# Graph transformer layer on one core: x @ loop weights + bias made ahead for all blocks, normalising moved to ScalarE

## What is computed

```python
k, q, v = (decomp(x, node_type, comp, basis) for ...)   # 4 basis matrices, mixed by node type
kt = einsum(k, relation_att)[edge_type, src];  vt = einsum(v, relation_msg)[edge_type, src]
e = (q[dst] * kt).sum(-1) * relation_pri[edge_type] * scale
a = softmax of e over the edges of each dst
agg = segment_sum(a * vt, dst)
out = relu(decomp(agg, node_type, comp_a, basis_a) + x @ loop_weight + bias)
return layernorm(x + out)
```

## Time and profile before

| what | value |
|---|---|
| median of 3 runs | 1438.44 us (1436.06 to 1438.98) |
| profiled execution, its own time | 1433.42 us |
| its span, first to last instruction | 1431.3 us |
| mean granted TensorE clock | 0.839 of full |
| TensorE busy | 1086.9 us (76%) |
| VectorE busy | 1007.8 us (70%) |
| GpSimd busy | 950.1 us (66%) |
| ScalarE busy | 746.5 us (52%) |
| table phase, queries | to about 197 us, to about 267 us |
| groups, first and last gather | 204.4 us, 1288.7 us |
| last addition to `agg`, end of the span | 1330 us, 1431.3 us |

### The profile page before, as it was taken

One profiled execution on the slowest core, in us unless ns is written; L12 is line 12 of the kernel. 1 busy time (PEld: TensorE's weight loads), 2 busy tenths in 40 slices (PEclk: granted clock), 3 DMA queues, 4 the chain that ended last, 5 costly groups with the idle time before them and its releaser, 6 DMA issues.

```text
span 1431.3 us, 29611 instructions
## 1 busy us (share of the span) xinstructions
PE 1086.9 (76%) x6749; PEld 892.8 (62%) x6750; DVE 1007.8 (70%) x2872; ACT 746.5 (52%) x1969; POOL 950.1 (66%) x941
## 2 busy tenths in 40 slices
PE   5999978777777676767777676777666777776797
PEld 2545544566767666666676666676656666665797
DVE  4797737677777676767777676767767676776686
ACT  2767746566555455556545455555445555540342
POOL 2567527747777777777777777777777777770441
PEclk9999989888888878878778788877878787876799
DMA  5989775323333333333333333333333333331022
GB/s 137 356 335 356 306 273 164 110 59 107 107 110 105 110 105 108 101 108 105 107 109 107 108 105 105 106 107 104 106 107 104 102 106 108 107 103 34 14 79 64
DMA packets 93799, 184.47 MB, mean 129 GB/s; under 512 B 26359, under 2 KB 59624, under 8 KB 87408
## 3 DMA queue, kind: packets, MB, share of 16 engines
q0 software_dynamic: 41680, 113.71, 27.7%
q1 hardware_dynamic: 49600, 69.49, 13.6%
q10 hardware_dynamic: 2400, 0.07, 0.1%
HBM read 127.71 MB, written 56.26 MB: 129 GB/s over the span
## 4 chain that ended last, share of the span: by engine, by line
POOL 31%; PE 26%; issue 19%; DVE 11%; DMA 5%; DVEq 4%; ACT 1%; ACTq 1%; SPq 1%; POOLq 0%
POOL kv L1161 31%; PE pb L1481 5%; DVE agg L720 3%; PE pb L1643 3%; PE pb L1592 3%; PE pb L1738 3%; PE pb L1502 3%; DVEq L691 3%; DMA kv<-table,idx_now 2%; PE pb L1552 2%; PE pb L1721 2%; DMA onehot<-in_x_dram 2%; PE pb L1618 1%; DVE work L685 1%; DVE kv L439 1%
## 5 line engine op out<-in xcount | busy, mean ns | idle before, releaser
L1161 POOL DMA_INDIRECT kv<-table,idx_now x832 | 814.6, 979 | 312.8 <-issue 246.9
L1643 PE MATMUL pb<-work,onehot 128*128 128x136 f32 x1664 | 340.4, 338 | 96.7 <-DVE agg L720 64.7
L720 DVE TENSOR_TENSOR agg<-agg,pb 128x136 f32 x832 | 241.8, 291 | 201.9 <-issue 72.0
L1643 PEld LDWEIGHTS pb<-work,onehot 128*128 128x128 f32 x1664 | 282.6, 236 | 120.0 <-issue 84.5
L1321 ACT ACTIVATE work<-pb 128x512 f32<-128x512 f32 x208 | 124.0, 596 | 331.4 <-PE pb L1581 331.4
L1592 PE MATMUL pb<-q_all,work 128*128 x1664 | 272.6, 317 | 0.7 <-ACT work L1321 0.6
L1592 PEld LDWEIGHTS pb<-q_all,work 128*128 128x128 f32 x1664 | 249.7, 229 | 7.9 <-issue 6.7
L1309 ACT ACTIVATE work<-lane,neg_lane 128x128 f32<-128x128 f32 x800 | 253.0, 390 | 0.0
L577 DVE TENSOR_TENSOR work<-kv,pb 128x512 f32<-128x512 f32 x208 | 142.3, 684 | 95.4 <-DMA kv<-table,idx_now 69.1
L1581 PE MATMUL pb<-ident,onehot 128*128 128x128 f32 x832 | 158.2, 322 | 67.0 <-ACT onehot L1315 63.7
L1581 PEld LDWEIGHTS pb<-ident,onehot 128*128 128x128 f32 x832 | 114.1, 165 | 88.0 <-ACT onehot L1315 62.9
(11 more groups left out here) (197 smaller groups left out, 1188.7 us busy)
## 6 DMA issues: line engine op xcount, KB each, us to landing
table<-kv SPq DMA_DIRECT2D x49, 1024.0 KB, 5.2
kv<-table,idx_now POOLq DMA_INDIRECT x832
seg<-item_bias SPq DMA_DIRECT2D x208, 16.0 KB
kv<-in_x_dram SPq DMA_DIRECT2D x8, 384.0 KB, 5.7
onehot<-in_x_dram SPq DMA_DIRECT2D x7, 384.0 KB
kv<-in_x_dram SPq DMA_DIRECT2D x6, 448.0 KB, 3.7
out_dram<-kv SPq DMA_DIRECT2D x6, 448.0 KB
onehot<-tile_blocks POOLq DMA_DIRECT2D x1, 784.0 KB, 8.8
```

Source lines behind the costliest of these rows:

```text
L720: v.tensor_tensor(a, a, PB[banks[i // 2 % len(banks)]][:, (i % 2) * 256:(i % 2) * 256 + W], ALU.add).then_inc(s_added, 1)
L1161: pool.indirect_dma_start(out=kv[:, o:o + 2 * D], out_offset=None, in_=table, in_offset=bass.IndirectOffsetOnAxis(ap=idx_now[par][:, i:i + ...
L1643: mm = t_.matmul(PB[banks[k % len(banks)]][:, u * 256:u * 256 + W], onehot[:, o:o + P], wv[:, b % WR, h * 2 + u, :], start=True, stop=True)
```

## The change

- `item_bias8`: at block 36 of the table phase SyncE copies `item_bias` eightfold from DRAM to DRAM, so that `segments` is one transfer instead of eight.
- `hold` waits for a semaphore that is long there instead of raising one; where a raise is kept it is `hold_apart`. The four squares raise `s_squares` once.
- x is loaded for all chunks in the last group, to one half of `kv` (places of the group before the last), each chunk when its places are weighed.
- `base` = x @ loop weights + bias, for all 49 blocks in 13 groups of 4, is kept in the queries' place `q_all`. TensorE turns 4 blocks of x into bank 0, ScalarE copies them to `spread`, TensorE multiplies into bank 2, ScalarE copies to `base`. Two turns stand in the last group's last batch, 3 groups before `turn_scores`, 4 single groups between the steps of the chain, 6 among the last sums, which use 3 banks.
- In the last stage TensorE only has the turned products and the four bases. VectorE adds `base` (first instruction) and then takes the relu and adds x (second). It makes the reciprocal and a `shift` = -mean x reciprocal; ScalarE normalises (scale and bias for each node) chunk n-1 between its copies 4, 5 and 6 and after copy 0 of the next; the last chunk is shared by both engines. `yo` has two buffers.

```diff
+    item_bias8 = nc.dram_tensor("item_bias8", [ITEMS // IL, H, IL * P], f32, kind="Internal").ap()
...
+        BASES_AT = [3, 1, 1, 1, 1]
+        BASES_FIRST = sum(BASES_AT)
-        LAST_SBANKS = [4, 5, 0, 1]
+        LAST_SBANKS = [4, 5, 3]
...
         def hold(engine):
+            engine.wait_ge(s_const, 8)
+        def hold_apart(engine):
             engine.sem_inc(s_hold, 1)
...
             def residual(ch, par):
                 for h, (c0, c1) in enumerate(((0, 4), (4, CB))):
-                    dve.wait_ge(s_layer_out, ch * 2 + h + 1)
-                    v.scalar_tensor_tensor(y[par][:, c0 * D:c1 * D], PB[4 + 2 * par + h][:, 0:(c1 - c0) * D],
-                                           0.0, x3[par][:, c0 * D:c1 * D], ALU.max, ALU.add)\
-                        .then_inc(s_residual, 1)
+                    dve.wait_ge(s_block_multiplied, ch * CB + c1)
+                    yc = y[par][:, c0 * D:c1 * D]
+                    v.tensor_tensor(yc, PB[4 + 2 * par + h][:, 0:(c1 - c0) * D],
+                                    base[:, bass.ds(ch * CN + c0 * D, (c1 - c0) * D)], ALU.add).then_inc(s_summed, 1)
+                    dve.wait_ge(s_summed, ch * 2 + h + 1)
+                    v.scalar_tensor_tensor(yc, yc, 0.0, x3[:, bass.ds(ch * CN + c0 * D, (c1 - c0) * D)],
+                                           ALU.max, ALU.add).then_inc(s_residual, 1)
...
-            def normalise(ch, par):
+            def inverse(ch, par):
                 dve.wait_ge(s_deviation, ch + 1)
-                v.reciprocal(rstd, rstd).then_inc(s_inverse_deviation, 1)
+                v.reciprocal(rstd[par], rstd[par]).then_inc(s_inverse_deviation, 1)
                 dve.wait_ge(s_inverse_deviation, ch + 1)
-                after(dve, s_stored, ch, 16, 0)
-                for c in range(CB):
-                    v.tensor_scalar(yo[:, c * D:(c + 1) * D], y[par][:, c * D:(c + 1) * D],
-                                    mv[:, c, 0:1], rstd[:, c:c + 1], ALU.subtract, ALU.mult)\
+                v.scalar_tensor_tensor(shift[par], mv[:, :, 0], -1.0, rstd[par], ALU.mult, ALU.mult)\
+                    .then_inc(s_shift, 1)
...
             def stage3(ch, par, first=False, final=False):
                 if not final:
                     products3(ch + 1, 1 - par)
                 if not first:
-                    normalise(ch - 1, 1 - par)
+                    inverse(ch - 1, 1 - par)
                 residual(ch, par)
...
         # sync
-                for h in range(H):
-                    sp.dma_start(seg3[h * IL:(h + 1) * IL, :, :], rows).then_inc(s_segments[par], 16)
+                sp.dma_start(seg3, item_bias8[bass.ds(g * IH, IH), :, :]
+                             .rearrange("i h (l e) -> (h l) i e", l=IL)).then_inc(s_segments[par], 16)
...
+                if n == STARTS_OUT_AT:
+                    sp.wait_ge(s_item_starts, 16)
+                    sp.dma_start(item_bias8, item_bias.rearrange("(j a l) e -> j a (l e)", a=1, l=IL)
+                                 .broadcast_to([ITEMS // IL, H, IL * P])).then_inc(s_starts_copied, 16)
...
-            sp.wait_ge(s_weighted, (GROUPS - 1) * NBATCH)
...
+            for ch in range(CHUNKS):
+                slots = -(-(ch + 1) * CN // (2 * D))
+                sp.wait_ge(s_weighted, (GROUPS - 2) * NBATCH + -(-slots // 4))
...
         # scalar
+            def copy_base(j):
+                many = min(4, BLOCKS - 4 * j) * D
+                act.wait_ge(s_base_made, j + 1)
+                a_.activation(base[:, j * 4 * D:j * 4 * D + many], PB[2][:, 0:many], ACT.Copy).then_inc(s_base_copied, 1)
+            copy_x3(0)
+            copy_x3(1)
+            for j in range(BASES_FIRST):
+                copy_base(j)
+                copy_x3(j + 2)
             exponentials(GROUPS - 1, 0)
...
+            def normalise(ch, par, use, cs):
+                act.wait_ge(s_shift, ch + 1)
+                after(act, s_stored[par], use, 16, 0)
+                for c in cs:
+                    a_.activation(yo[par][:, c * D:(c + 1) * D], y[par][:, c * D:(c + 1) * D], ACT.Identity,
+                                  bias=shift[par][:, c:c + 1], scale=rstd[par][:, c:c + 1]).then_inc(s_normalised, 1)
...
                 for c in range(1, CB):
                     copy_products(ch, par, c)
-                    if c == 3 and not first:
-                        deviation(ch - 1)
-                    if c == XAT + 1 and not final:
-                        copy_x3(ch + 1, 1 - par)
+                    if c == 3 and use_prev is not None:
+                        deviation(ch - 1, 1 - par)
+                    if c >= 4 and use_prev is not None:
+                        k = 2 * (c - 4)
+                        normalise(ch - 1, 1 - par, use_prev, range(k, k + 2))
                 if not final:
                     copy_products(ch + 1, 1 - par, 0)
+                if use_prev is not None:
+                    normalise(ch - 1, 1 - par, use_prev, range(CB - 1, CB))
...
         # tensor
+            def make_base(j):
...
+                    pe.wait_ge(s_base_copied, j)
+                pe.wait_ge(s_xT3_copied, j + 1)
+                for u in range(min(4, BLOCKS - 4 * j)):
+                    o = PB[2][:, u * D:(u + 1) * D]
+                    t_.matmul(o, xT3[:, j % 2, u, :], Wl[:, :], start=True, stop=False)
+                    mm = t_.matmul(o, ones3, bias3, start=False, stop=True)
+                mm.then_inc(s_base_made, 1)
...
+            bases(BASES_AT[0])
             turn_scores(g, 1)
             sums(g - 1, 0, 12)
+            bases(BASES_AT[1])
             turn_ends(g)
...
             for k in range(2 * NBATCH):
                 sums(g, 1, k, LAST_SBANKS)
+                if k % 2 and made[0] < X3:
+                    bases(1)
...
-                    t_.matmul(o, xT3[par][:, c * P:(c + 1) * P], Wl[:, :], start=False, stop=False)
-                    mm = t_.matmul(o, ones3, bias3, start=False, stop=True)
```

More of the change, by code:

```diff
@@ L211, in graph_transformer_layer @@
         s3 = Space(kv, 2 * G * 2 * D)
-        x3 = [s3.take(CN) for _ in range(2)]
-        xT3 = [s3.take(CN) for _ in range(2)]
+        x3 = s3.take(BLOCKS * D)
+        base = q_all
+        assert s3.at <= G * 2 * D
+        s3 = Space(kv, 2 * G * 2 * D, at=G * 2 * D)
         y = [s3.take(CN) for _ in range(2)]
-        yo = s3.take(CN)
+        yo = [s3.take(CN) for _ in range(2)]
         anT = s3.take(2 * NB * P).rearrange("p (r b n) -> p r b n", r=2, b=NB)
@@ L220, in graph_transformer_layer @@
         mv = s3.take(CB * 2).rearrange("p (c k) -> p c k", c=CB)
-        rstd = s3.take(CB)
+        rstd = [s3.take(CB) for _ in range(2)]
+        shift = [s3.take(CB) for _ in range(2)]
         eps = s3.take(1)
+        xT3 = spread
+        X3 = -(-BLOCKS // 4)
         h3 = Space(onehot, 2 * G * P)
@@ L302, in graph_transformer_layer @@
         s_added = sem("s_added")
-        s_x3_loaded = [sem(f"s_x3_loaded{r}") for r in range(2)]
+        s_x3_loaded = [sem(f"s_x3_loaded{ch}") for ch in range(CHUNKS)]
         s_factors = sem("s_factors")
@@ L318, in graph_transformer_layer @@
         s_inverse_deviation = sem("s_inverse_deviation")
+        s_shift = sem("s_shift")
         s_normalised = sem("s_normalised")
-        s_stored = sem("s_stored")
+        s_stored = [sem(f"s_stored{r}") for r in range(2)]
         block = ctx.enter_context(nc.Block())
@@ L1391, in _ @@
             rise_exp(GROUPS - 1)
-            copy_x3(0, 0)
-            for b in range(2, NBATCH):
-                exponentials(GROUPS - 1, b)
+            exponentials(GROUPS - 1, 2)
+            exponentials(GROUPS - 1, 3)
+            for j in range(BASES_FIRST, X3):
+                copy_base(j)
+                if j + 2 < X3:
+                    copy_x3(j + 2)
+                if j - BASES_FIRST < NBATCH - 4:
+                    exponentials(GROUPS - 1, 4 + j - BASES_FIRST)
+            assert X3 - BASES_FIRST >= NBATCH - 4
             def copy_products(ch, par, c):
@@ L1402, in copy_products, with deviation @@
                     .then_inc(s_products_copied, 1)
-            def deviation(ch):
+            def deviation(ch, par):
+                after(act, s_normalised, ch - 1, CB, 0)
+                hold(act)
                 act.wait_ge(s_mean_var, ch * CB + CB)
-                a_.activation(rstd, mv[:, :, 1], ACT.Sqrt, bias=eps[:, 0:1]).then_inc(s_deviation, 1)
-            def stage3(ch, par, first=False, final=False):
+                a_.activation(rstd[par], mv[:, :, 1], ACT.Sqrt, bias=eps[:, 0:1]).then_inc(s_deviation, 1)
@@ L1426, in _ @@
[L1426 removed]
+                stage3(it * 2, 0, it - 1)
+                stage3(it * 2 + 1, 1, it)
+            stage3(CHUNKS - 1, 0, CHUNKS // 2 - 1, final=True)
+            deviation(CHUNKS - 1, 0)
+            normalise(CHUNKS - 1, 0, CHUNKS // 2, range(3, CB))
         @block.tensor
```

177 lines of the change are left out of this document (97 added, 80 removed).

## The result

| | before | after |
|---|---|---|
| median (range), us | 1438.44 (1436.06 to 1439.76) | 1453.24 (1447.62 to 1458.62) |
| profiled execution, us (span) | 1433.42 (1431.3) | 1450.35 (1448.3) |
| mean granted clock of TensorE | 0.839 | 0.847 |
| last gather issued | 1288.70 | 1285.79 |
| from there to the last addition's end | 41.25 | 49.35 |

The kernel became slower: ratio 1.0110, 95% interval 1.0081 to 1.0139. The forecast was 1455.8 for the median and 1450.8 for the profiled execution. The rows from the last gather on add up to the difference of the spans: -2.9 + 8.1 - 2.8 + 13.9 + 0.7 = +17.0.

The account below looks back on a forecast made before the run. GpSimd's gathers were taken to bound 302 to 1289 us; front -1.9, tail +9 and last stage +10.3 sum to +17.4, giving 1450.8 us profiled and 1455.8 median. The range was 1438 to 1466.

Parts of the forecast that it names:

- Front: The stretch to 302 us: a wait of 5.4 us goes, the eightfold copy costs 3.5; in all -1.9 us.
- The wait goes: -5.4: TensorE's 5.40 us wait at 205.3 for the second chunk of x vanishes, as SyncE issues two loads, not 16.
- I take 3.5: Cost in us of the eightfold DRAM-to-DRAM copy at block 36 of the table; bounds 0 and 10.
- The gathers cover them: Between 302 and 1289 us GpSimd's gathers set the pace, so saved issues and increments are costed at nothing.
- Tail: 1289 to 1330 us: bases on TensorE delay the scans and lengthen the sums' loop; +9 us, bounds +4 and +14.
- Last stage: 1330 us to the end: a new loop of waits between engines outweighs the work saved; +10.3 us.
- The circle: Last stage, each chunk: ScalarE's copies wait for the shift, it for products, they for the residual; 15.05 us against 12.1.
- rival 1: Last stage: either the clock stays up or the shift isn't held, stage +2.3 or +3.1; time 1448; chance 0.22.
- Rival 3: The tail takes the bases into TensorE's idle time, +4 us there; time 1450.8; chance 0.12.
- Rival 2: Last stage runs at VectorE's own pace, 10.75 us a chunk; stage -10.0, time 1435.5; chance 0.14.
- Rival 4: The eightfold copy stalls the table, +10 us in place of +3.5; time 1462.3; chance 0.08.

Follow-up runs that it names:

- early shift: The kernel after, with reciprocal and shift of chunk n-1 made on VectorE before its big products for chunk n+1; 1442.35 us, ratio 1.0048.
- filled pause: The kernel after, with 36 unread transposes on TensorE ahead of block 5 in chunks 1 to 5 of the last stage; 1444.24 us, ratio 1.0062.
- moved bases: The kernel after, with one base ahead of sums 11, none before the scores' turn, eight in the last sums' loop; 1447.99 us, ratio 1.0078.
- the last two: Two kernels on a slower chip: the kernel after with only TensorE's and ScalarE's last-stage order changed (1.0094), or with old segment loads behind the second chunk (1.0072).

## Why the prediction was right, step by step

**Front, -1.9 forecast, -2.9 measured: misses that cancel.** "The wait goes: -5.4" was right as a wait and too small as a price: 9.0 us on its own, since the pause also lowered the clock for the blocks behind it. I had that very effect in the earlier trace rows and used it only for the last stage. In the kernel after GpSimd's wait fell by 13.1 (17.66 to 4.52). From the first gather to the end of that wait are 97.6 us before and 84.5 to 88.6 in the eleven profiles in which TensorE's wait is gone (those on the slow chip left out), so some 4 us of it vary from one execution to the next. "I take 3.5" for the copy was too small as well: 6.5 in the kernel after, 8.0 and 6.8 in the two other comparisons. The estimate has one stall, and the trace has two. The store of block 40 is issued 8.0 us behind that of block 39 (3.3 before), where ScalarE waits 5.62 us. The store of block 42 is issued 5.3 behind that of block 41 (3.2 before); TensorE's clock was 0.50 from 175 to 180, behind the first stall, but the second wasn't taken apart. "The gathers cover them" holds for the issues saved, but the loop of the gathers, costed at nothing, took 3.7 us more (from 295.46 to 1285.79, before from 302.05 to 1288.70). The three terms are -13.1, +6.4 and +3.7.

**Tail, +9 forecast, +8.1 measured.** The mechanism was right (TensorE in front of the scans: groups 2.24 us apart, forecast 2.2), its split wrong: the scan is 7.4 later against the last gather, forecast 5.2, and all that follows adds 0.7, forecast 3.8. The sums' loop costs 0.3 a batch for six batches, 1.8, and not 3, and the rest is likely the clock: from 1300 to 1330 it was 1.00 after, and 0.50, 0.87 and 0.64 in three windows before. That share wasn't tried on its own.

**Last stage, +10.3 forecast, +11.8 measured.** The circle exists, in the links and the order foretold, and each was cut on its own: the shift's place (early shift), its holding (one operand in PSUM), the clock (filled pause), ScalarE's part (normalising on VectorE). Link by link, chunk 4 to 5: residual 2.9 (2.7), products 5.14 (5.15), reciprocal and shift 1.68 (1.85), shift to residual 6.3 (5.35). The last was mis-sized: without the clock it is 4.2 for 3.75, and the clock takes 2.1 for 1.6. The hold isn't tied to the shift: in the fifth turn VectorE's products had it.
Where the trace of before had only one operand price, a per-partition bias, the trace of after has both operands:

```profile
L1453 ACT ACTIVATE kv<-kv 128x128 f32<-128x128 f32 x46 | 20.1, 483 | 21.7 <-DVE kv L865 21.7
...
L1328 ACT ACTIVATE work<-lane,neg_lane 128x128 f32<-128x128 f32 x800 | 253.0, 390 | 0.0
```

0.483 us with two pointer operands, 0.390 with one: 0.093 between them. The rule that I weighed and left out of the sum, the Trainium skill's 0.09 us for each such operand (ScalarE: Activation LUTs, "What ACT_TABLE_LOAD costs"), agrees with this. Its 0.4 a circle is as large as what 4.2 exceeds 3.75 by, but the operands aren't all of that: with the pause filled, ScalarE takes 2.6 us from its first normalising to the end of copy 6 (1403.14 to 1405.75), where I had 2.5.
The total came near partly by luck: the first period was 12.85 and not 15.05, because there the clock stayed up (the block took 1.16 us at 1363.75), and the four behind it are 0.65 us longer than forecast. That it stayed up was chance: in the kernel with the moved bases the same pause of 2.89 us was followed by a block at half clock, the first period is 14.3, and the stage is 86.6.
On the clock the Trainium skill (TensorE: Matmul & The Clock Gate, "HAM oscillation — how this bites in real kernels") has every burst after a long enough stall start low; here the four turns with pauses of 3.5 to 4.3 us did. The first, with one of 2.9 us, didn't, and with the moved bases the same pause did; with the operand in PSUM a pause of 2.3 us was followed by a block at full clock (1.16 us) and then by one of 1.9 us. So the length of the pause alone doesn't decide it.

**The rivals.** Of rival 1's two savings neither came: the clock fell in four of five turns, and the shift was held in four of five. Rival 3's +4 for the tail was 8.1. Rival 2, VectorE's own pace of 10.75, named the right number but not what it takes: it needs three moves that the change doesn't make, and then gives 10.9 to 11.8. I had left out the second circle altogether; hidden behind the first it cost the forecast nothing, but it would have spoiled rival 2 even with a free shift, at 13.7. Rival 4's stall of the table (+10) was about as far off as my 3.5: 6.5.

## What to carry to other kernels

Work moved to an engine that has room is not free when that engine also feeds the critical one in order: write down, for one turn of the loop, who waits for whom through every in-order engine, and look for a second circle behind the first. A pause of TensorE can cost its own length and the half clock behind it: a wait of 5.4 us was worth 9 here, and the clock behind the pause of each turn 2.1. A single profile can have some microseconds of chance in it (6 in the start of the table, 1.4 in the first turn of the last stage), so a stage is best compared from a mark just ahead of the edit. Where a small instruction reads two SBUF tensors beside a long GpSimd one, one operand in PSUM or an earlier place can be worth more than the instruction's own work.

## What the runs showed that I had not expected

- The holding by GpSimd hits long instructions too: in the three kernels with the early shift, the residual's second instruction (two SBUF tensors, 512 columns) reaches 1.49 us, for 0.69 in the kernel after, when GpSimd's product still runs; with the shift's operand in PSUM it reaches 1.11.
- A copy of 3.5 MB from DRAM to DRAM, issued among table stores, delayed the first gather by 6 to 8 us. The issues that it saves (8.61 us down to 2.21) aren't on the path once the second chunk is issued first.
- The kernel before took 1437 to 1439 us (medians) beside all other kernels and 2039 us beside the last two. In the two kernels profiled there, the last stage is as elsewhere, GpSimd's own time for a gather is no longer (958 and 961 ns, for 979 and 984 before and after here), but it waits 613 and 620 us for VectorE's weighing, and VectorE and ScalarE wait for what is called remote. The cause wasn't found.
